# Weighted edge sums into one accumulator instead of two, each add behind the add just ahead of it

## What is computed

```python
a = exp(logits - segment_max(logits, dst)[dst])
out = segment_sum(a[:, :, None] * h[src], dst) / segment_sum(a, dst)
```

## Time and profile before

| | |
|---|---|
| median of 3 runs | 7781.81 us (7779.54 to 7785.45) |
| the profiled execution | 7779.64 us |
| its span, first to last instruction | 7777.4 us |
| mean granted TensorE clock | 0.789 of full speed |
| instructions | 91180 |
| busy: PE, POOL, DVE, ACT | 5083.8, 3616.8, 2832.3, 1496.1 us |
| the three `edge_sum` loops, first to last add | 908.6 to 1135.3, 2943.8 to 3167.6, 5371.1 to 5597.8 us |

### The profile page before, as it was taken

The page is one execution under the profiler, slowest core; times in us unless marked ns, Lnnn a source line. Parts: engine busy times, 40 slices in busy tenths (PEclk is TensorE's granted clock), DMA queues, the critical chain, the costliest instruction groups (busy, mean ns, idle before and its releaser), DMA issues. The chain is left out here.

```text
span 7777.4 us, 91180 instructions
## 1 busy us (share of the span) xinstructions
PE 5083.8 (65%) x22571; PEld 4050.9 (52%) x22572; DVE 2832.3 (36%) x6312; ACT 1496.1 (19%) x3806; POOL 3616.8 (47%) x3066
## 2 busy tenths in 40 slices
PE   0588578991045548799999463334734788688566
PEld 0577456771023435488888462333533666576444
DVE  3311572120023437510101113115722577477553
ACT  0000373330000008300000120004711222122221
POOL 0377475777737757200000214775622477577300
PEclk9655698995577769899999785556968899889787
DMA  6699452111119976344443454885534588588300
GB/s 232 200 264 264 150 193 34 1 1 1 1 36 315 338 267 219 117 125 126 126 138 105 157 156 136 235 236 164 181 102 136 157 265 263 176 260 262 104 0 21
DMA packets 994978, 1218.07 MB, mean 157 GB/s; under 512 B 272564, under 2 KB 784413, under 8 KB 994809
## 3 DMA queue, kind: packets, MB, share of 16 engines
q1 hardware_dynamic: 411241, 536.49, 23.5%
q0 software_dynamic: 291808, 364.37, 18.3%
q10 hardware_dynamic: 291760, 315.27, 11.6%
HBM read 840.14 MB, written 374.71 MB: 156 GB/s over the span
## 5 line engine op out<-in xcount | busy, mean ns | idle before, releaser
L597 POOL DMA_INDIRECT logit_rows<-tab,src_a x832 | 793.9, 954 | 540.3 <-POOLq L93 287.5
L597 POOL DMA_INDIRECT max_rows<-tab,src_a x832 | 786.6, 945 | 382.3 <-issue 231.2
L1222 POOL DMA_INDIRECT counts<-put_n,put_at x400 | 795.8, 1990 | 303.8 <-issue 256.5
L716 PE MATMUL ps_a<-msg,sel 128*128 128x264 f32 (+2 forms) x2496 | 631.7, 400 | 117.6 <-DVEq L648 68.1
L1543 POOL DMA_INDIRECT moe_x<-xn,slot x100 | 97.2, 972 | 1219.0 <-POOLq L93 1189.2
L716 PEld LDWEIGHTS ps_a<-msg,sel 128*128 128x128 f32 x2496 | 453.7, 191 | 295.3 <-DVE acc L662 85.8
L516 PE MATMUL ps_t<-ident,rows 128*128 128x128 f32 x300 | 69.4, 342 | 806.1 <-DVE rows L477 800.0
L1033 PE MATMUL ps_a<-hl,blocks 128*128 128x256 f32 x2600 | 578.0, 379 | 0.5 <-PE ps_a L1033 0.3
L1033 PEld LDWEIGHTS ps_a<-hl,blocks 128*128 128x128 f32 x2600 | 491.9, 190 | 78.1 <-issue 13.6
L1987 DVE TENSOR_TENSOR_SCAN run<-same,run,ps_t 128x512 f32<-128x512 bf16 x416 | 508.5, 1265 | 1.7 <-PE ps_t L1915 0.9
L597 POOL DMA_INDIRECT logit_rows<-tab_kv,src_a x416 | 396.2, 953 | 241.8 <-issue 116.7
(11 more groups left out here) (437 smaller groups left out, 8981.1 us busy)
## 6 DMA issues: line engine op xcount, KB each, us to landing
slot_rows<-logit_rows ACTq DMA_DIRECT2D x312, 512.0 KB
edge_rows<-slot_rows SPq DMA_DIRECT2D x312, 512.0 KB
blocks<-counts SPq DMA_DIRECT2D x390, 320.0 KB
seg_rows<-back ACTq DMA_DIRECT2D x208, 512.0 KB
counts<-zeros ACTq DMA_DIRECT2D x26, 1600.0 KB, 17.5
locs<-loc_slots SPq DMA_DIRECT2D x312, 128.0 KB
att<-in_attr_t SPq DMA_DIRECT2D x1248, 32.0 KB
wf<-in_L_ffn_W SPq DMA_DIRECT2D x57, 512.0 KB
```

The source lines that it names most:

```text
L597: self.nc.gpsimd.indirect_dma_start(out=self.rows[:, (n % Q) * Q + j, :], out_offset=None, in_=table, in_offset=bass.IndirectOffsetOnAxis( ...
L716: nc.tensor.matmul(ps_a[:, n % 8, 0:C], sel[:, b % 2, j, :], rhs, start=True, stop=True).then_inc(summed, 1)
L1222: nc.gpsimd.indirect_dma_start(out=g.counts, out_offset=bass.IndirectOffsetOnAxis(ap=g.put_at[:, j:j + 1], axis=0), in_=g.put_n[:, j:j + 1 ...
```

## The change

The second accumulator goes, with its memset and the final addition. All adds go into `acc`. Since two neighbouring adds may now have the same tile, add n waits until n adds are written, that is for the add just ahead.

```diff
         ring = Ring(nc, ph, g, "edge", D)
-        odd = sb("odd", [P, NT, C], F32)
         sel = sb("sel", [P, 2, Q, P], F32)
...
                 v.memset(acc[:, :, 0:C], 0.0).then_inc(zeroed, 1)
-                v.memset(odd[:], 0.0).then_inc(zeroed, 1)
-                dve.wait_ge(zeroed, 2)
+                dve.wait_ge(zeroed, 1)
                 dve.sem_inc(added, 8)
...
                     for j in range(Q):
                         n = b * Q + j
                         dve.wait_ge(summed, i * W + n + 9)
-                        dve.wait_ge(added, i * W + n + 7)
-                        to = (odd if j % 2 else acc)[:, ds(tiles[j], 1), 0:C].rearrange("p a c -> p (a c)")
+                        dve.wait_ge(added, i * W + n + 8)
+                        to = acc[:, ds(tiles[j], 1), 0:C].rearrange("p a c -> p (a c)")
                         v.tensor_tensor(to, to, ps_a[:, n % 8, 0:C], ALU.add).then_inc(added, 1)
...
                 body(LOOPS - 1, False)
-                dve.wait_ge(added, STEPS + 8)
-                v.tensor_tensor(acc[:, :, 0:C], acc[:, :, 0:C], odd[:], ALU.add).then_inc(zeroed, 1)
```

## The result

The changed kernel takes 7923.94 us (median of 4 runs, 7923.43 to 7930.76) where the kernel before, run beside it, takes 7780.68: 1.0186 times as long, 95% interval 1.0168 to 1.0204, or 143 us. Forecast were 7925 and +144 us. The profiled execution has a span of 7921.2 us.

A forecast was written before the change was run, and what follows sets the result against it. The loop over two `msg` buffers bounded the kernel; VectorE would become the bound. Added 62.0 us a stage, 186 in three, less 41.6 for memset and whole-tile add, gave +144 us: 7925 us, range 7870 to 7985.

The forecast's parts named there:

- The bound before: In the edge_sum stages, the loop between GpSimd's products and TensorE's matmuls over two `msg` buffers bounds: 4.34 us per eight adds.
- The hand-over, 0.04 + 0.07 + 0.10: On VectorE behind each add: wait released, address instruction begins, add starts; 0.21 us together, so a step of 0.64 us.
- the lower bound from edge_logits: Dependent instruction there starts 0.15 us after the end it waits for, without extra wait instruction: step 0.58, total 7869 us.
- the upper one from the earlier trace: Catch-up stretch of adds chained at distance two: 0.26 us behind an add, step 0.69, total 7972 us.
- The pauses: Steps between blocks of four adds, where tile numbers are loaded: 0.75 us within a loop body, not growing with the change.
- The loop's branch: Step from one loop body's last add to the next body's first: 1.17 us, passed 24 times a stage, not growing.
- Front and end: Removed per three stages: memset of `odd` with idle time ahead, 20.5 us; whole-tile add at the end, 21.0 plus 0.1 ahead.
- The last addition: Closing sum of the total: profiled execution 7779.64 us plus 144 makes 7924, median 2.2 higher, stated as 7925.
- The overlap and the rule: Adds of 0.43 us start 0.34 apart, so they overlap; by the skill's rule the wait would be free, only -41.6 us.
- The free and the cheap wait: Two rivals for the new wait: free, 7740 us, chance 0.05; or hand-over 0.03 us, step 0.46, 7757 us, chance 0.05.
- The third rival: In the stages TensorE's clock gives way and TensorE bounds: 7980 us at mean clock 0.85, 8112 at 1.2 GHz; chance 0.12.
- the signs: Expected in the profile after: adds 0.64 us apart, TensorE and GpSimd waiting for the add, hardly an add waiting for TensorE.

## Why the prediction was right

- *The bound before.* Right, and shown: four `msg` buffers took 76 us off the kernel before, with VectorE's part unchanged. One reading was loose: in the earlier trace rows TensorE's block is released by ScalarE's copy into `msg` (L697), which waits for the same matmuls as the product does, and not by GpSimd's product.
- *The hand-over, 0.04 + 0.07 + 0.10.* Right, and each part is now seen at distance one: 0.21 us behind each add, step 0.64. It had been put together from three places, since no row showed it whole. Taking one part away each (wait instruction, address instruction) or lengthening one gave 0.57, 0.53 and 0.66. The value in the middle held because it was counted in this line's own instructions; the lower bound from edge_logits turned out to be the case without the wait instruction, and the upper one from the earlier trace rows still had a busy engine in it.
- *The pauses.* 0.75 was right. The loop's branch took 1.16, 1.16 and 1.03 us on the mean in place of 1.17, and one pause of the body in the second stage 0.87. That these two cancel, so that the three stages take 862.0 us for 863.4, is luck: with one instruction more ahead of the loop they take 871.3.
- *Front and end.* -20.5 and -21.1 were forecast; the traces before and after have -20.5 and -21.0. The runs that change one of them alone give 24 for the front, within a margin of more than ten, and 20.5 for the end.
- *The last addition.* 7779.64 + 144 + 2.2 is 7926 and not 7925, which changes nothing.
- *The overlap and the rule.* The step goes from 0.34 at best to 0.64 with the wait, and with two accumulators the wait alone cost 190 us. The Trainium skill says in "VectorE: DVE Perf Modes", section "The DRAIN you can't avoid", of eight chained copies that a semaphore after each costs nothing extra. This doesn't carry over to these adds: they raise a semaphore each in both kernels, and what costs is to wait for that of the add just ahead. The prediction also holds the overlap of the earlier trace rows against that section of the Trainium skill. It overlooked that the section itself adds that a next operation that isn't held starts earlier, which the 0.34 us agree with.
- *Rivals.* The free and the cheap wait would have shown as steps of 0.44 to 0.46. The clock stayed at 0.99 to 1.00: TensorE, though waiting in between at each slot, kept it. The third rival's premise did not come about in the profile either: TensorE's busy share was to fall to 0.72 and went up to 0.94 (269.9 of 288 us), since its records get longer where it waits.
- *What I got wrong in the signs.* I had written that hardly an add would be put down to waiting for TensorE. The profile puts 302.2 of 333.3 us down to it, more than before. Whoever had gone by that sign would have called the prediction wrong and looked for the fault at TensorE.

## What to carry to other kernels

Two accumulators in turn are no luxury where the result of one short operation is waited for by the next: the wait costs the overlap of the two (here 0.09 us of 0.43) and the hand-over behind the first (here 0.21 us). The hand-over depends on the chain of sequencer instructions between the wait and the work: 0.10 us with the wait instruction alone, 0.14 with the address instruction alone, 0.21 with both. Count those instructions, and let the wait sit on the last one; here the choice of a semaphore's starting value alone was worth 73 us in the three stages. But do this only for the engine that is the bound: with two accumulators the same edit gave nothing, and two more buffers elsewhere gave 76 us.

## What was not expected of the hardware

The profile's releaser of an idle time can be the fulfilled one of two waits: 302 us were put down to matmuls that had ended 4.2 us earlier (median of each stage 4.16 to 4.26). Test a releaser by the lead of the producer, or by shortening it.

The same loop with the same waits isn't equally fast everywhere. Single places of the body took 0.11 us more in one kernel or stage than in the next, and the branch 1.03, 1.16 or 1.28 us; one instruction more ahead of the loop moved them, up to 6 us a stage. With effects of some 10 us in a kernel of this kind one should compare steps in the trace and not totals.
